# A vision layer with routed experts: x laid out on 128 partitions, another pooling product, and new work orders

## The reference, cut to what matters

```python
# x: (64, 12, 224, 224) float32
pooled = x.reshape(64, 12, 14, 16, 14, 16).sum(axis=(3, 5))       # 196 tokens of an image, 12 channels
h = einsum('bcij,ce->bije', pooled, channel_weights)              # 12544 tokens of 192
h = h + attention(layernorm(h), w_qkv, w_proj, b_proj)            # 12 heads, relu(1 + qk + qk^2/2), normalised
flat = layernorm(h)
top_w, top_i = top_k(softmax(flat @ router_w.T), 2)               # 2 of 8 experts for each token
for e in range(8):
    w_e = sum(top_w * (top_i == e))
    out = out + w_e * (gelu(flat @ w1[e] + b1[e]) @ w2[e] + b2[e])   # w1: 192x768, w2: 768x192
h = h + out
```

## Time and profile before

| | |
|---|---|
| median of 3 runs | 1551.34 us (1547.84 to 1552.79) |
| the profiled execution | 1550.52 us |
| its span, first to last instruction | 1548.7 us |
| busy in the span | PE 1280.8 us, DVE 1008.8 us, POOL 716.1 us, ACT 617.3 us |
| granted TensorE clock, mean | 0.906 |
| bytes moved | 323.11 MB |

### The profile page before, as it was taken

How to read it: one execution, slowest core, us unless ns; L and a number is a source line. 1 busy time by engine, 2 the same in 40 slices (tenths; PEclk the granted TensorE clock), 3 DMA queues, 4 the chain that set the end, 5 groups by cost and what they waited for, 6 DMA issues and landing times.

```text
span 1548.7 us, 28863 instructions
## 1 busy us (share of the span) xinstructions
PE 1280.8 (83%) x7793; PEld 1131.5 (73%) x7793; DVE 1008.8 (65%) x3793; ACT 617.3 (40%) x1203; POOL 716.1 (46%) x557
## 2 busy tenths in 40 slices
PE   4465457089898989899898989898989999998996
PEld 3455346068787878787787878787878888887885
DVE  1887877457776868586868686777683433455553
ACT  1021221045353545353434343434343544555554
POOL 0004302514747474647474647465646463432332
PEclk9995555589999999899999899999999999999999
DMA  6979679657889898989898989898963666666766
GB/s 159 255 187 246 195 196 238 174 170 187 243 236 249 221 261 215 263 201 266 214 264 219 260 218 264 220 253 229 238 168 87 182 174 139 156 171 177 188 181 179
DMA packets 194052, 323.11 MB, mean 209 GB/s; under 512 B 25337, under 2 KB 158570, under 8 KB 193962
## 3 DMA queue, kind: packets, MB, share of 16 engines
q1 hardware_dynamic: 150858, 280.98, 63.2%
q0 software_dynamic: 43104, 41.25, 16.1%
HBM read 267.20 MB, written 54.95 MB: 208 GB/s over the span
## 4 chain that ended last, share of the span: by engine, by line
PE 56%; DVE 22%; issue 8%; POOL 5%; DMA 4%; ACT 3%; SPq 2%; DVEq 0%; POOLq 0%; ACTq 0%
PE ps L933 16%; PE ps L961 15%; DVE red L1006 8%; PE ps L760 5%; POOL rows_d L589 4%; PE ps L880 4%; PE ps L904 3%; PE ps L905 3%; DMA w1r<-L_ffn_w 3%; PE ps L828 3%; PE ps L869 2%; PE ps L859 2%; PE ps L847 2%; DVE topi L1132 1%; DVE newton L1072 1%
## 5 line engine op out<-in xcount | busy, mean ns | idle before, releaser
L961 PE MATMUL ps<-w2r,hid 128*128 128x192 f32 x2520 | 453.8, 327 | 19.0 <-ACT hid L703 19.0
L600 POOL DMA_INDIRECT result<-ys,ridx x210 | 326.7, 1556 | 279.2 <-ACT ys L736 181.8
L1006 DVE TENSOR_REDUCE red<-xbuf 112x14 f32<-112x448 f32 x768 | 422.1, 608 | 51.0 <-PE ps L828 49.0
L961 PEld LDWEIGHTS ps<-w2r,hid 128*128 128x128 f32 x2520 | 411.8, 190 | 35.1 <-ACT hid L703 24.6
L589 POOL DMA_INDIRECT rows_d<-rows,sloti x256 | 246.6, 963 | 313.9 <-issue 176.3
L703 ACT ACTIVATE hid<-ps,b1s 128x512 f32<-128x512 f32 (+1 forms) x380 | 230.7, 617 | 380.8 <-PE ps L933 268.6
L610 POOL TENSOR_TENSOR w1l<-w1r,w1h 128x768 fp32r<-128x768 f32 x74 | 146.9, 2078 | 218.9 <-ACT w1h L715 218.6
L933 PE MATMUL ps<-xh,w1h 128*128 128x512 f32 (+1 forms) x380 | 173.7, 457 | 28.4 <-ACT hid L703 15.9
L1230 DVE TENSOR_TENSOR xl<-ps,xh 128x512 fp32r<-128x512 f32 (+1 forms) x64 | 38.2, 596 | 211.6 <-ACT xh L722 211.5
L715 ACT CAST w1h<-w1r 128x768 fp32r<-128x768 f32 x128 | 106.1, 829 | 105.9 <-PE ps L933 59.7
L933 PE MATMUL ps<-xh,w1l 128*128 128x512 f32 (+1 forms) x380 | 140.6, 370 | 0.0
(11 more groups left out here) (169 smaller groups left out, 1795.3 us busy)
## 6 DMA issues: line engine op xcount, KB each, us to landing
xbuf<-x SPq DMA_DIRECT2D x128, 1176.0 KB, 9.2
w1r<-L_ffn_w SPq DMA_DIRECT2D x130, 384.0 KB, 4.8
w2r<-L_ffn_w SPq DMA_DIRECT2D x65, 576.0 KB, 6.0
xr<-rows_d SPq DMA_DIRECT2D x42, 402.0 KB, 3.2
result<-h1s SPq DMA_DIRECT2D x32, 294.0 KB
xr<-rows_d SPq DMA_DIRECT2D x23, 201.0 KB, 2.4
rows_d<-rows,sloti POOLq DMA_INDIRECT x256
rows_d<-pad SPq DMA_DIRECT2D x9, 402.0 KB, 5.6
```

The lines of the kernel that those rows point to most:

```text
L600: pool.indirect_dma_start(out, bass.IndirectOffsetOnAxis(ap=ridx[:, b, n:n + 1], axis=0), ys[:, b, n, :], None, compute_op=ALU.add).then_i ...
L961: last = mm(yout(g, b, n), hid[:, m % 3, cols], w2r[:, b, m, :], start=False, stop=m == MC - 1 and n % 2 == 1)
L1006: V.tensor_reduce(red[:, k // 2, CH * (k % 2) + c, :], xbuf[:, k % XSLOTS, c, :].rearrange("p (r j w) -> p j r w", r=2, j=G), AX.XY, ALU.a ...
```

## The change

- x is laid out by the host in another way: 14 chunks a step, each 128 partitions of 5376 contiguous bytes, 7 buffers. A partition holds one of 8 pairs of image rows of a patch for one of 16 (image, channel) pairs; 3 groups of 16 make the 48 of a step.
- A P now reduces 128x672 to 128x21. There are 28 P a step.
- S1 on PE is 6 products (2 halves of the tokens by 3 groups, summed in PSUM) of `red` (128x98 as weights) with `mixg` (128x96), and gives what S2's product gave. The 14 products of line 828, ACT's copy to `pT` and S2's 2 products go. The next step's first P waits for S1's products (`s_mix`). DVE's S2 is as it was.
- Setup makes `repeat` (DVE) and `mixg` (3 products on PE, a copy on DVE), loads two x chunks ahead of the weights, does 18 P at named places and 10 among the scores (before: 4 for each score), and splits b2 earlier.
- `STEP_ALONE`, `ORDER` and `TAIL_ORDER` are new.

```diff
-CHUNKS = 2 * IPS
-XSLOTS = 4
+CHUNKS = 14
+XSLOTS = 7
+HALVES = 2
+SUMS = NSUM // (CHUNKS * HALVES)                 # NSUM = 3 * 196
-STEP_ALONE = """P P S1 P S2 S3 P P P P P P P P S4 P P P P S5 P P P P P P P P P P P S6.0 S6.1 S6.2 S6.3 P S7.0 P P S7.1 P P P
-    S8.0 S8.1 P P S8.2 S8.3 S10 R V.0 V.1 P V.2 V.3 S11 P P P S9 P P P P Q0 P P P P Q1 Q2 P Q3 P""".split()
+STEP_ALONE = """S1 S2 P P S3 P P P P P P P P P P P S4 S5 P P P P S6.0 S6.1 S6.2 S6.3 S7.0 P P S7.1 S8.0 S8.1 S8.2 P S8.3 P
+    S10 R V.0 V.1 V.2 P V.3 P P S11 P S9 Q0 Q1 P P Q2 P Q3""".split()
 ORDER = [
-    """P S1 M2 P L J P X0 M3 S2 P W0 N0 P X1 P N1 N2 P N3 K M4 P S3 I M5 S4 P P P P P P N4 N5 W1 P S5""".split(),
-    """M0 P P <A S6.0 S6.1 <Y N0 M1 P M2 X0 M3 S6.2 S6.3 W0 X1 N1 L P P S7.0 P N2 P P W1 N3 M4 M5""".split(),
-    """M0 P S7.1 S8.0 P P <J S8.1 M1 P <N4 <I <N5 <Y P <K P P M2 X0 P S8.2 S8.3 N0 P S10 W0 R N1 N2 L <A M3 X1 M4
-       V.0 S11 V.1 S9 V.2 P P P P Q0 V.3 P W1 P I Q1 M5 N3 N4 N5 K P Q2 J Q3 P""".split(),
-    """M0 <A P <Y P P P P P M1 P P""".split(),
+    """L S1 M2 S2 X0 M3 P J K X1 N0 P N1 N2 P S3 S4 P N3 S5 M4 P W0 P M5 P S6.0 Y N4 P N5 S6.1""".split(),
+    """M0 M1 M2 <W1 <I P N0 S6.2 S6.3 N1 X0 N2 P W0 P M3 X1 S7.0 P M4 P S7.1 P S8.0 <A L J K S8.1 W1 A S8.2 P M5 P
+       P I N3 S8.3 S10 R Y N4 N5""".split(),
+    """M0 M1 M2 P X0 N0 N1 V.0 P W0 M3 P S11 N2 V.1 P S9 X1 V.2 W1 L Q0 V.3 Q1 Q2 P P M4 M5 I N3 N4 P J K P""".split(),
+    """M0 Q3 <A P M1 <Y P <N5 P""".split(),
 ]
 TAIL_ORDER = [
-    """N0 M2 X0 W0 M3 X1 N1 L J M4 M5 W1""".split(),
-    """M0 M1 <N2 <Y M2 <N3 <K <N4 <N5 <I N0 N1 X0 M3 L X1 J M4 N2 W0 W1 M5 <A N3 N4 N5 I""".split(),
-    """M0 <Y <A M1 M2 X0 W0 N0 M3 X1 <K M4 M5 N1 N2 L J K A N3 N4 I W1 N5 Y""".split(),
+    """N0 M2 X0 W0 M3 X1 L J K N1 M4 M5 W1""".split(),
+    """M0 M1 <N2 <Y M2 <N3 <N4 <N5 <I N0 N1 X0 M3 L X1 N2 J K M4 I W0 W1 M5 <A N3 N4 N5""".split(),
+    """M0 <Y <A M1 M2 X0 W0 N0 M3 X1 N1 M4 M5 N2 L J K A N3 N4 I W1 N5 Y""".split(),
...
             def load_chunk(s, k):
+                sp.dma_start(xbuf[:, k % XSLOTS].rearrange("p h n w -> p (h n w)"),
+                             x[bass.ds(s * (CHUNKS * 128) + k * 128, 128)]).then_inc(d_x[k % XSLOTS], 16)
...
+            for k in range(2):
+                load_chunk(0, k)
             for dst, src in weights:
                 sp.dma_start(dst, src).then_inc(d_w, 16)
...
-            def S1(s):                                                     # ACT
-                act.wait_ge(s_psum1, s + 1)
-                copy(pT[:].rearrange("p i j -> p j i"), ...)
...
+            set_wait(pe, "dve", "mix")                                     # PE, setup
+            for g in range(GROUPS):
+                last = mm(ps[:, 7, g * 2 * IPS * C:(g + 1) * 2 * IPS * C], repeat[:, g * 128:(g + 1) * 128], mix,
+                          start=True, stop=True)
...
             def S1(s):                                                     # PE
                 pe.wait_ge(s_pooled, s * PARTS + PARTS)
-                for jj in range(G):
-                    last = mm(ps[0:IPS * C, 0, jj * G:(jj + 1) * G], lhs[:, :, jj], const("rowsel", ROWP),
-                              start=True, stop=True)
-                last.then_inc(s_psum1, 1)
-            def S2(s):
-                pe.wait_ge(s_pT, s + 1)
                 for hf in range(2):
-                    last = mm(ps[0:TOK, 1, hf * 96:(hf + 1) * 96],
-                              pT[:, hf * G // 2:(hf + 1) * G // 2, :].rearrange("p i j -> p (i j)"), mix,
-                              start=True, stop=True)
+                    for g in range(GROUPS):
+                        o = g * NTOK + hf * TOK
+                        last = mm(ps[0:TOK, 1, hf * 96:(hf + 1) * 96], red[:, o:o + TOK], mixg[:, g],
+                                  start=g == 0, stop=g == GROUPS - 1)
                 last.then_inc(s_mix, 1)
...
             def P(s, p, first=False):                                      # DVE
-                k, c = p // CH, p % CH
+                k, h = p // HALVES, p % HALVES
                 if p == 0 and not first:
-                    dve.wait_ge(s_psum1, s + 1)
+                    dve.wait_ge(s_mix, s + 1)
...
-                V.tensor_reduce(red[:, k // 2, CH * (k % 2) + c, :],
-                                xbuf[:, k % XSLOTS, c, :].rearrange("p (r j w) -> p j r w", r=2, j=G),
-                                AX.XY, ALU.add).then_inc(s_pooled, 1)
+                V.tensor_reduce(red[:, p * SUMS:(p + 1) * SUMS], xbuf[:, k % XSLOTS, h], AX.X,
+                                ALU.add).then_inc(s_pooled, 1)
...
+            pool_first(4)                                                  # DVE, setup: before the wait for weights
...
+            pool_first(2)                                                  # after "router"
...
+            pool_first(4)                                                  # before "amat"
...
+            pool_first(8)                                                  # before the scores
+            left = PARTS - 18
             for h in range(HEADS):
-                for p in range(PARTS * h // HEADS, PARTS * (h + 1) // HEADS):
-                    P(-1, p, first=True)
+                pool_first(left * (h + 1) // HEADS - left * h // HEADS)
                 set_wait(dve, "act", f"factors{h}")
```

More of the change, by code:

```diff
@@ L48 @@
 NT = 2 * IPS
-ROWP = IMG // 2
+EIGHTH = PATCH * PATCH // 8
+GROUPS = IPS * C // 16
+NSUM = GROUPS * NTOK
 U = C + 1
@@ L89 @@
 _W = 0
-for _n, _w in (("ident", 128), ("rowsel", G), ("mixinit", 2 * IPS * C), ("spread", IPS * C), ("block", IPS * C),
+for _n, _w in (("ident", 128), ("mixinit", 2 * IPS * C), ("spread", IPS * C), ("block", IPS * C),
                ("self", 2 * NF), ("selg", 4 * NF),
@@ L206, in vit_layer @@
         padi = sb("padi", [128, TP], I32)
-        xbuf = sb("xbuf", [ROWP, XSLOTS, CH, 2 * IMG])
-        red = sb("red", [ROWP, IPS, C, G])
-        pT = sb("pT", [IPS * C, G, G])
+        xbuf = sb("xbuf", [128, XSLOTS, HALVES, SUMS, EIGHTH])
+        red = sb("red", [128, NSUM])
+        mixg = sb("mixg", [128, GROUPS, 2 * IPS * C])
         prod = sb("prod", [TOK, NT, C])
@@ L291, in vit_layer @@
             "pool": ["zeros", "fills", "pad"],
-            "dve": ["copies", "cwc", "router", "cwT", "rtT", "gram", "wide", "mix", "amat"]
-                   + [f"score{h}" for h in range(HEADS)] + ["score", "b2"],
+            "dve": ["copies", "cwc", "router", "cwT", "rtT", "gram", "wide", "mix", "mixg", "b2", "amat"]
+                   + [f"score{h}" for h in range(HEADS)] + ["score"],
             "act": ["resT", "logits", "values", "qk", "bmat"] + [f"factors{h}" for h in range(HEADS)],
-            "pe": ["turned", "gram", "wide", "blocks", "logits", "values", "qk", "amat", "bmat"]
+            "pe": ["turned", "gram", "wide", "blocks", "mixg", "logits", "values", "qk", "amat", "bmat"]
                   + [f"factors{h}" for h in range(HEADS)],
@@ L450, in _ @@
             ]
+            for k in range(2):
+                load_chunk(0, k)
             for dst, src in weights:
                 sp.dma_start(dst, src).then_inc(d_w, 16)
-            for k in range(XSLOTS):
+            for k in range(2, XSLOTS):
                 load_chunk(0, k)
             for k in range(CHUNKS):
-                sp.wait_ge(s_pooled, CH * (k + 1))
+                sp.wait_ge(s_pooled, HALVES * (k + 1))
                 load_chunk((k + XSLOTS) // CHUNKS, (k + XSLOTS) % CHUNKS)
@@ L469, in P @@
             def P(s, p):
-                k = p // CH + XSLOTS
-                if p % CH == CH - 1 and (k < CHUNKS or steps_left[0]):
+                k = p // HALVES + XSLOTS
+                if p % HALVES == HALVES - 1 and (k < CHUNKS or steps_left[0]):
                     sp.wait_ge(s_pooled, s * PARTS + PARTS + p + 1)
@@ L746, in prime @@
                 M(0, 0, 1)
[L748 removed]
+            schedule(act, {"S3": S3, "S4": S4, "S5": S5, "S7": S7, "S8": S8, "V": V, "M": M, "W": W,
                            "X": X, "Y": Y}, prime=prime)
@@ L782, in _ @@
                                      start=True, stop=True))
+            set_wait(pe, "dve", "mix")
+            for g in range(GROUPS):
+                last = mm(ps[:, 7, g * 2 * IPS * C:(g + 1) * 2 * IPS * C], repeat[:, g * 128:(g + 1) * 128], mix,
+                          start=True, stop=True)
+            given("pe", "mixg", last)
             set_wait(pe, "dve", "rtT")
@@ L1017, in link, with pool_first @@
                 dve.wait_ge(s_dvs, n_set[0])
+            pooled = iter(range(PARTS))
+            def pool_first(n):
+                for _ in range(n):
+                    P(-1, next(pooled), first=True)
             dve.wait_ge(d_cst, 16)
+            V.tensor_copy(repeat.rearrange("p (k u) -> p k u", u=8),
+                          const("ident", IPS * C)[:, 0:IPS * C].unsqueeze(2).to_broadcast([IPS * C, IPS * C, 8]))
             V.tensor_copy(base[:], const("base"))
@@ L1040, in _ @@
```

(9 more changed lines are left out.)

30 lines of the change are left out of this document (9 added, 21 removed).

## The result

The changed kernel takes 1507.2 us (median of 4 runs, 1503.7 to 1508.0); the kernel before, on the same chip, 1552.1 us (4 runs, 1547.8 to 1554.1). The ratio is 0.971, 95% interval 0.968 to 0.974: 45 us faster, where 93 were forecast. The profiled execution spans 1505.2 us at a mean granted clock of 0.904.

What follows compares the result with a forecast made beforehand. DVE bounds steps alone; PE, waiting for DVE's pooling, those with tiles. 1550.5 us less 24.1 up to step 4, 66 in eleven steps and 3 in the last gives 1457.4, with 0.8 added 1458; range 1438 to 1503.

Steps and rivals of the forecast that it cites:

- The size of a P: Each new DVE reduction takes 0.752 us for 0.526 before; with 28 for 48, 4.2 us less DVE a step.
- it doesn't do what it says: Rival: a P of 0.90 us saves DVE nothing; some 1488 us, within the range, no chance of its own.
- Setup: Before the steps: the first S1 starts at 59.5 to 60 us instead of 69.3, a gain of 9.4 us.
- Steps alone: Steps 0 to 3, without tiles: 50.1 us each for 54.4, 4.3 less; four steps give 17.2 us.
- So the wait falls from 4.4 to about 1 us: Middle steps, PE ahead of S1: behind S9 DVE has some 10 us of work, PE some 9.
- The clock at 1.00 around it: Around S1 in middle steps: the clock stays high, so M2's five products take 1.16 us instead of 2.43.
- The sum of a middle step: Steps with tiles: 69.5 us when quiet, 70.2 in the mean; 6.0 less each, 66 us over eleven steps.
- POOL's loop: Middle steps: POOL's queue of 32.5 us and PE's stretch from M0 to M5, 36.7, close in 69.2 us.
- The last step and the tail: The last step, which has no P, gains 3 us; the tail with its changed order gains 0.
- DMA becomes the bound: Rival, chance 0.14: DMA at a share of 0.94 holds middle steps at 72.5 us; 1486 us in all.
- The waits of PE come back elsewhere: Rival, chance 0.18: tight lists make PE wait at other places; only 2.0 us a step saved, 1502 us.
- Slower: POOL's loop opens: Rival, chance 0.05: PE's stretch from M0 to M5 takes 12 us more; middle steps of 81 us, 1576 us.

Runs made afterwards that it cites:

- both_fillers: The changed kernel with dead PE products in steps 4 to 15, eight ahead of S1's wait and five ahead of S4's: 1465.2 us, ratio 0.947.
- filler: The changed kernel with eight dead PE products of 192 columns ahead of S1's wait in steps 4 to 15: 1490.7 us, ratio 0.961.
- the versions where both waits are mended: Changed kernel, three P moved ahead of S11, N3 ahead of S4, M4 ahead of S5: 1455.3 us; with five dead products ahead of S4 too: 1448.6 us.
- the last version: The changed kernel with three P ahead of S11, N3 ahead of S4, M4 ahead of S5, and five dead products ahead of S4's wait: 1448.6 us.

## Why the prediction was wrong, step by step

The direction and most terms were right. The time was 49 us off, because one step of the sum failed and pulled a second with it.

- **The size of a P** (0.752 us forecast): 0.755, from the five in 3.87 us less one tail of 0.85, over 4. Right, and the rival "it doesn't do what it says" falls.
- **The size of S1** (1.4 us at the high clock, 2.5 at the low): 1.28 and 2.31. Right.
- **Setup** (S1 at 59.5 to 60): 57.8. The weights land 3.2 us later than before where 5.3 were forecast; that is the difference.
- **Steps alone** (50.1 us): 51.2. Of the 4.3 us forecast, 3.2 came. PE waits 9.2 us ahead of S1 there, so DVE still sets these steps. The balance up to S1 of step 4 is 21.8 us for 24.1.
- **PE's work in a middle step** (66.3 us): 65.4 at a clock of 1.00. Right, to the good side.
- **"So the wait falls from 4.4 to about 1 us":** this is the step that failed. It fell to 2.9. The forecast let DVE and PE leave S9 together and compared what stands behind it, some 10 us against some 9. Both sizes are about right (DVE from 579.7 to 589.1, 9.4 us; PE from 575.7 to 586.3 with 1.3 of waiting, 9.3). But DVE came to S9 3 us after PE's product of it. By moving W0 the new list put a low part of w1 beside S11, which stands ahead of S9 and wasn't counted, and DVE's small instructions lost 3.2 us, 2.4 of them there. Where only W0 is moved away from there, the wait is 1.64 us, and where the P are moved, 0.6.
- **"The clock at 1.00 around it":** this followed from the step before and failed with it. The prediction had priced the clock at the seam (S1 and M2) and taken that price as saved. With two waits left, of 2.9 and 1.0 us, the lower level costs 3.6 us in the mean step (74.5 less the 70.9 of `both_fillers`), where the forecast had none. The wait of 0.9 ahead of S4 was forecast to 0.1 us, and counted as 0.9. The clock that may follow it was left out: with that wait open and S1's closed a step is 73.4 us in the mean (`filler`) instead of 70.9 (`both_fillers`), 2.5 us more.
- **The sum of a middle step**: 70.2 forecast, 74.5 measured. The 4.3 us are 3.6 of clock and 0.7 of the rest (70.9 for 70.2). In a quiet step at full clock (70.6 for 69.5) PE idles 5.2 us where the terms left 1.9 and POOL's loop 1.3 more, and works 0.9 less.
- **POOL's loop** (69.2 us): not reached in the kernel after. In the versions where both waits are mended, the quiet steps take 69.0 to 69.3 us and PE waits for POOL's low part. There 1.1 us of PE work more didn't lengthen the step. The computed loop is the next bound, as far as these rows can tell; it wasn't changed by itself.
- **The last step and the tail** (3 and 0): 3.7 together. Right.

The rivals: *DMA becomes the bound* is refuted. The share is 0.83 in a step of 70.6 us and 0.84 in one of 69.3, where the 0.88 of the prediction's counterargument was for 70.2, and a chunk lands in 7.2 us. (At 0.94 its step is 68.0 / 0.94 = 72.3 us, not 72.5.) The formula of the Trainium skill's page "DMA: Bandwidth & Descriptors" (section on the anatomy of a DMA) as serial time, 50 us for 14 chunks in a row, isn't seen: a chunk takes 7.2 us to land, so 14 in a row would be 101 us, and a step of 51.2 us has all 14; they overlap, and DVE waits 2.1 us for x in the whole kernel. The Trainium skill fits the formula to DMAs that GpSimd issues; these are issued by SyncE. *The waits of PE come back elsewhere* (1502) was the case that came true, by its price and in part by its kind, and I gave it 0.18. It was right that waits stay, and wrong where: the main one is the old one. *Slower: POOL's loop opens* is refuted: POOL is as busy as before (44.9 us a step) and PE doesn't wait for it.

What would have found it: the trace of before had the sign. Its `pend` was stalled in eleven of the twelve steps with tiles, for 1.15 to 2.69 us where its median is 0.16. In step 5 it ended at 434.19, and a low part on POOL at 434.15 (`pend` over the whole trace, as ns least, median, most; then step 5):

```profile
L1207 DVE TENSOR_TENSOR pend<-avail,cons x65: 145/164/2691, 286.8 to 1533.7; 128x8 f32<-128x8 f32 x65
```

```profile
432.95 1.24 DVE L1207 TENSOR_TENSOR pend<-avail,cons 128x8 f32<-128x8 f32 x1
...
431.77 2.38 POOL L610 TENSOR_TENSOR w1l<-w1r,w1h 128x768 fp32r<-128x768 f32 x1
```

When a list of names is moved against another engine's, it should be read for pairs that may not overlap. The Trainium skill has the rule, on the page "SBUF — State Buffer", section "Who interferes with whom": copies, casts and `tensor_scalar` on VectorE can take a port pair shared with GpSimd, a `tensor_tensor` with two inputs in SBUF contends with what GpSimd reads, whoever starts first holds the pair to the end of its instruction, and a `tensor_reduce` on trn2 never contends. The traces here agree in three of the four: 2.57 and 2.54 us for a CAST and a TENSOR_SCALAR of 98x8 that need 0.17, 0.93 and 1.12 for TENSOR_TENSORs that need 0.17 and 0.29, all to within 0.16 us of the end of POOL's instruction, and five reductions unchanged at 3.88. Who starts first they don't settle: that CAST's record starts 0.12 us ahead of POOL's (574.23 and 574.35), and it is DVE that waits; starts on POOL are rough in the profile. Read beside the lists it gives a term of 2.4 us a step for S11 behind W0, and the price of the clock in the earlier trace rows would have stayed in the sum with it.

## What to carry to other kernels

Price an idle stretch of PE as itself and the lower clock that may follow, and find out with a handful of dead products whether the second is there: here it was 3.6 us of a 74.5 us step, against waits of 2.9 and 1.0. When such products help, look which wait has shrunk: in the last version it was another than the one they stood at. When small instructions are placed by a list, keep the long elementwise instructions of POOL beside reductions of DVE and not beside its chain of small ones; a timeline in which two ends agree to 0.05 us finds such a pair. A layout and an order that were changed together have to be tried apart: the same order cost 41 us with one layout and gave some 20 with the other.
